# A graph network kernel: the leaky unit of its second edge stage written with tanh, and a group's softmax work spread over two steps

## The reference

```python
def _smooth_leaky(x, alpha=0.2):
    return 0.5 * (1 + alpha) * x + 0.5 * (1 - alpha) * x * (2.0 * jax.nn.sigmoid(x) - 1.0)
ms = src_s[edge_src] + dst_s[edge_dst]          # 64 scalars of an edge
mv = src_v[edge_src] + dst_v[edge_dst]          # 32 vectors of 3
w = h @ rw3 + roff                              # weights of the edge, from an MLP
ds, dv = ...                                    # products of w, ms, mv and the edge's direction Y1
ls, lv = _eq_lin(ds, dv, lin_ws, lin_bs, lin_wv)
alpha = ls[:, :H * A].reshape(e, H, A)          # 8 heads of 8
a = jnp.einsum('ehk,hk->eh', _smooth_leaky(alpha), alpha_dot)
amax = jax.ops.segment_max(a, edge_dst, num_segments=n)
a = jnp.exp(a - amax[edge_dst])
a = a / (jax.ops.segment_sum(a, edge_dst, num_segments=n)[edge_dst] + 1e-12)
ns = jax.ops.segment_sum(vs * a[..., None], edge_dst, num_segments=n)   # and nv likewise
```

## Time and profile before

| | |
|---|---|
| time, median of 3 runs | 10474.15 us (10468.27 to 10480.74) |
| the profiled execution's own time | 10483.94 us |
| its span | 10482.1 us |
| PE busy | 8818.0 us (84%) |
| DVE busy | 7895.4 us (75%) |
| ACT busy | 5096.8 us (49%) |
| POOL busy | 6671.5 us (64%) |
| second edge stage: first and last `e_m` | 5672.5 and 9745.3 us |

### The profile page before, as it was taken

How to read it: one execution, slowest core, us unless ns; L and a number is a source line. 1 busy time by engine, 2 the same in 40 slices (tenths; PEclk the granted TensorE clock), 3 DMA queues, 4 the chain that set the end, 5 groups by cost and what they waited for, 6 DMA issues and landing times. The chain is left out here.

```text
span 10482.1 us, 192677 instructions
## 1 busy us (share of the span) xinstructions
PE 8818.0 (84%) x34728; PEld 5222.1 (50%) x34728; DVE 7895.4 (75%) x15400; ACT 5096.8 (49%) x9268; POOL 6671.5 (64%) x4771
## 2 busy tenths in 40 slices
PE   0888888888888799999996888888888888888588
PEld 0444444444444222322233666676666667676333
DVE  3277777777777588888896888888888888888465
ACT  0176666666666311111112555555555555555355
POOL 4478888888888788888884445444544544444232
PEclk5599999999999899999997999999999999999699
DMA  5588888888888899999993444444444444444222
GB/s 199 180 162 168 167 165 166 166 167 166 168 165 167 171 224 227 230 224 230 225 235 97 124 130 127 124 129 124 126 124 130 126 126 128 125 126 125 67 76 58
DMA packets 1081323, 1616.13 MB, mean 154 GB/s; under 512 B 218498, under 2 KB 831885, under 8 KB 1025357
## 3 DMA queue, kind: packets, MB, share of 16 engines
q1 hardware_dynamic: 755862, 1273.87, 44.1%
q0 software_dynamic: 325056, 338.58, 20.5%
HBM read 1533.80 MB, written 444.07 MB: 189 GB/s over the span
## 5 line engine op out<-in xcount | busy, mean ns | idle before, releaser
L442 POOL DMA_INDIRECT sums<-e_total,e_place x1568 | 2494.2, 1591 | 592.7 <-DMA sums<-e_total,e_place 330.8
L1933 POOL DMA_INDIRECT e_rows<-TS,e_at x1568 | 1540.0, 982 | 2086.2 <-DVE e_m L1961 1334.2
L579 PE MATMUL ps<-e_win,e_pick 128*128 128x448 f32 x3136 | 1335.7, 572 | 168.3 <-DVE e_u L476 127.8
L579 PEld LDWEIGHTS ps<-e_win,e_pick 128*128 128x128 f32 x3136 | 614.1, 201 | 917.3 <-issue 834.0
L2124 PE MATMUL ps<-e_win,e_pick 128*128 128x160 f32 x3136 | 620.7, 324 | 349.3 <-DVE e_pick L1951 281.9
L2261 ACT ACTIVATE e_dT<-ps 128x512 f32<-128x512 f32 x1176 | 660.1, 598 | 372.2 <-PE ps L2135 352.0
L1094 POOL TENSOR_TENSOR n_zv<-n_zv,n_ast 128x1536 f32<-128x1536 f32 x200 | 751.4, 3757 | 134.5 <-DMA n_zv<-in_x_groups 122.7
L2124 PEld LDWEIGHTS ps<-e_win,e_pick 128*128 128x128 f32 x3136 | 487.9, 202 | 564.0 <-issue 403.3
L1299 PE MATMUL ps<-n_z,w_uss 128*64 128x512 f32 x1600 | 746.7, 610 | 22.9 <-DVE n_z L1142 21.9
L2261 ACT ACTIVATE e_oT<-ps 128x512 f32<-128x512 f32 x784 | 468.2, 597 | 603.0 <-PE ps L2163 488.7
L2135 PE MATMUL ps<-ident,e_d 128*128 128x128 f32 x4704 | 648.3, 274 | 125.4 <-ACT e_dT L2261 125.0
(11 more groups left out here) (439 smaller groups left out, 20048.0 us busy)
## 6 DMA issues: line engine op xcount, KB each, us to landing
e_win<-T SPq DMA_DIRECT2D x1568, 168.0 KB
n_z<-in_x_groups SPq DMA_DIRECT2D x400, 512.0 KB
n_zv<-in_x_groups SPq DMA_DIRECT2D x800, 192.0 KB
TOT<-e_tot SPq DMA_DIRECT2D x392, 352.0 KB, 2.6
e_row<-in_src_rows SPq DMA_DIRECT2D x98, 1024.0 KB
e_local<-LR SPq DMA_DIRECT2D x196, 512.0 KB
e_row<-in_dst_rows SPq DMA_DIRECT2D x98, 1024.0 KB
e_win<-TD SPq DMA_DIRECT2D x1568, 60.0 KB
```

Of the source, the lines that this page charges most:

```text
L442: pool.indirect_dma_start(sums[c], bass.IndirectOffsetOnAxis(ap=place[:, r % 4, c:c + 1], axis=0), total[:, r % 4, c, 0:MSG0], None, compu ...
L579: pe.matmul(g[:, c, :], pick[:, p, R * c:R * c + R], win[:, s, c, :], start=True, stop=True).then_inc(spread, 1)
L1933: pool.indirect_dma_start(rows[:, p, 0, c, :], None, TS, bass.IndirectOffsetOnAxis(ap=at[:, gp, col:col + 1], axis=0)).then_inc(rows_here[ ...
```

## The change

Five things change.

1. The silu of `results` becomes a tanh of half the argument; DVE's combination becomes (tanh + 1.5) times alpha instead of 0.25 alpha plus silu, and the constant weight is scaled by 0.4 instead of 0.8. The count and the shapes of the instructions stay.
2. One load of the table set `exp_and_others` stands before the stage's loop on ACT.
3. DVE: `scans` goes from `r % 4 == 0`, behind `weigh`, to `r % 4 == 1`, behind `sums` and ahead of `results`. `shift` goes to behind `weigh` of that same step.
4. PE: `logits_up` stays at the end of `r % 4 == 0`; `tops_down` goes to the next step, behind its last `turn`.
5. ACT: `weigh_up` goes, within `r % 4 == 1`, from ahead of `results` to behind the second `keep_totals`, with only the last `keep` of the step behind it. SP's load of `e_dh`, which waits for the scans, goes from `r % 4 == 1` to `r % 4 == 2`.

```diff
-            step(dve.tensor_scalar(W["ad"][:], W["ad"][:], 0.8, None, ALU.mult))
+            step(dve.tensor_scalar(W["ad"][:], W["ad"][:], 0.4, None, ALU.mult))
...
-                        if r % 4 == 1 and not i.before(4) and not (final and r == 5):
+                        if r % 4 == 2 and not i.before(4) and not (final and r == 6):
                             gate(sp, k)
                             sp.wait_ge(scanned, i.groups(0))
                             load_dh(1 - r // 4, t + r // 4)
...
-                    dve.scalar_tensor_tensor(out=silu[:, p], in0=alpha4, scalar=0.25, in1=silu[:, p], op0=ALU.mult, op1=ALU.add
+                    dve.scalar_tensor_tensor(out=silu[:, p], in0=silu[:, p], scalar=1.5, in1=alpha4, op0=ALU.add, op1=ALU.mult
...
                         if more:
                             sums(after)
+                        if r % 4 == 1 and not i.before(5):
+                            scans(i)
                         if not i.before(1):
                             results(i.plus(-1))
                         if more:
                             weigh(after)
-                        if r % 4 == 0 and not i.before(4):
-                            scans(i)
+                        if r % 4 == 1 and not i.before(5):
                             shift(i)
...
                         turn(i, 2)
+                        if r % 4 == 1 and not i.before(5):
+                            tops_down(i)
                         map_scalars(i)
...
                             logits_up(i)
-                        if r % 4 == 0 and not i.before(4):
-                            tops_down(i)
...
-                    act.activation(silu[:, p], alpha4, ACT.Silu).then_inc(outs, 1)
+                    act.activation(silu[:, p], alpha4, ACT.Tanh, scale=0.5).then_inc(outs, 1)
...
-                        if r % 4 == 1 and not i.before(5):
-                            weigh_up(i)
                         if not i.before(1):
                             results(i.plus(-1))
                         keep(i, 0)
...
                         if not i.before(6):
                             keep_totals(i, 1)
+                        if r % 4 == 1 and not i.before(5):
+                            weigh_up(i)
                         keep(i, 4)
 
+                act.preload_act_table_set("exp_and_others")
```

## The result

The changed kernel takes 10090.11 us (median of 4 runs, 10076.11 to 10095.01), the kernel before, on the same chip, 10471.21 us. The ratio is 0.9626 with a 95% interval of [0.9606, 0.9646]: 381 us less. The forecast was 9961 us with a range of 9930 to 10060, so the direction was right and the time lies 30 us above the range. The profiled execution took 10076.11 us.

A forecast was written before the change was run, and what follows sets the result against it. DVE, with three waits a group, was taken to bound the stage. A group goes from 41.73 to 36.49 us, 5.24 less in each of 98 groups, so 10474 - 513 = 9961 us, range 9930 to 10060.

The forecast's parts named there:

- price of POOL's product: POOL's 1.26 us product waits for the exponential and ends 0.9 us into the next step, before the gathers; cost 0.
- Table loads: ACT in the loop: both loads of each group go, 2.57 us a group, which alone doesn't give the gain.
- Rival C: Scans' waits only moved, so only the table loads' 2.57 us a group came out: 10222 us, chance 0.04.
- ACT's results, scans, maxima: DVE's waits for ACT's copy (310.9 us in all), before the scans (1.22) and before the subtraction (0.56) all go.
- `weigh_up` on ACT: ACT stands 1.8 us for the subtraction; the last `keep` runs 0.6 into the next step, hidden by 0.5 us.
- Rival B: ACT's hold makes the last `keep` late for PE, which would stand 0.8 us a group: 10040 us, chance 0.07.
- the test in the prediction's last part: Step behind scans over 8.64 us refutes the forecast: slow matmuls mean rival A, PE waiting for `e_oT` Rival B.
- Clock: PE idle once a group, 1.5 to 1.7 us behind the long step; no fall 0, one a group 147 us.
- rival A: Clock falls behind PE's new gap: 10108 us if in every group, 10010 if in a third; chance 0.14.
- Rival D: PE loses its clock and doesn't regain it at once; two half-clock steps a group: 10874 us, chance 0.03.
- least group: Scan block on DVE at busy times less overlap, about 1.7 us, gives 25 us more: 9936 us.

The follow-up runs named there:

- subtraction early: Changed kernel with the subtraction of the maxima (`shift`) moved ahead of `weigh`; 10032.09 us, ratio 0.9564; run again 10037.93 us, 0.9557.
- selections first: Kernel with the subtraction early, and `e_pick` also ahead of `e_q` in the scans' step; 10010.93 us, ratio 0.9541; run again 10027.43 us, 0.9545.

## Why the prediction missed

- **What failed is the price of POOL's product.** The prediction wrote that it "is 1.26 us long and ends 0.9 into the next step, ahead of the next gathers", and costed it at 0 because no one waits for it. The place was nearly right (it ends 1.19 into the next step). That it runs beside `e_m` was read off as overlap, and it is none: 1.06 us x 98 = 104 us. In the kernel before, the product met only a part of a short instruction (0.2 us a group, L2027), and I didn't look at which instructions it would meet at its new place. With the product cut to an eighth the group is 36.61 us and the stage 83 us shorter, and the ratio of 0.9552 on 10474.15 us is 10005 us: inside the forecast's range, 44 us above the forecast.
- **Table loads: right that they go, and that they alone don't bring the gain.** Their share is smaller still: 158 us of the stage alone and 7 with the new order, so that the two halves of the change overlap almost wholly, as long as `e_m` is held. Rival C, in which only the loads count, is refuted from both sides.
- **ACT's results, scans, maxima: right.** All three waits of DVE are gone, the step with the scans is 10.57 and 10.44 us in the two groups of a pass against 10.57, and the plain steps have means of 8.60 to 8.65. DVE is above 90% busy.
- **`weigh_up` on ACT: right.** ACT is idle 1.35 and 1.66 us before the exponential in the two groups shown (1.8 forecast), and the copy behind it ends 0.26 into the next step, well before the second half of the window matmuls at 1.52. The list of waits puts PE's gaps down to that `keep` (209.3 us, with a further gap of 0.7 us in the step behind), which the times of `e_pick` contradict. Rival B had the price of what happened and the wrong cause: the test in the prediction's last part, a long step with PE waiting for `e_oT`, would by the list of waits have named B wrongly. Such a test should have been made on the instruction that grew longer.
- **Clock: right for this kernel, but with luck.** PE's gap was forecast at 1.5 to 1.7 us; it is 1.44 in one group and up to 1.81 in the other, with no fall and a clock of 1.00. The forecast took no fall because a gap of 1.5 to 1.7 us is nearer to the 1.12 us of the kernel before behind which the clock stays at 1.00 than to the 3.28 us with a single transpose (7019.38 to 7022.66) behind which it is 0.63. That was weak: the kernel with the subtraction early has falls from 1.84 us on (1 and 12 in 98 groups), which is nearer to 1.12 as well. So rival A holds for the neighbours; the 1.5 us a fall in it are (1 - 0.63) of the 4.00 us of the earlier trace rows. Rival D, the slower one, did not come: in that kernel a fall costs 2.1 us once, and not several steps.
- **Range.** It had room for losses by clock and by ACT, both worked out, and none for two engines that get in each other's way. With the 104 us the same sum gives 10065, 25 below the median measured. (Its least group, with a scan block of 1.7 us instead of 1.93, is worth 23 us and not 25; that changes nothing.)

By stage the account closes: 411.1 us of gain measured, 104 us of held `e_m`, 515 together against a forecast of 513. The median is 14 us above the profiled execution, whose own gain is 10483.94 - 10076.11 = 408; the stages that the change doesn't touch vary by that much, and I can't say why.

## What to carry to other kernels

When an instruction of POOL is moved, look at what DVE does at the new place, not only at who waits for its result: here the product cost nothing beside `e_d`, which reads PSUM (0.55 us as ever), and 1.06 us beside `e_m`, with two tensors in SBUF (1.88 instead of 0.82), and `e_pick` (0.77 instead of 0.48) shows that one tensor in SBUF can be enough. A step forecast from rows of idle time should also list which pairs of instructions become neighbours. And where two edits each remove the same wait (here the loads and the order), test each alone before crediting either; an edit that only shortens a step can lose part of its gain to the clock if the hole in PE's work stays, as the tanh alone did with 86 falls against 42.

## What the runs showed of the hardware

- POOL's product and the DVE instructions with two SBUF inputs that met it excluded each other. `e_m` ends 0.68 to 0.69 us behind the product for products of 0.51, 0.97 and 1.44 us, `e_q` 0.55 us behind it (subtraction early); `e_d`, which reads PSUM and SBUF, keeps its 0.55 us beside it.
- `e_pick`, one bf16 tensor in SBUF and f32 out, is held as well (0.77 us instead of 0.48). Alone, its 512 elements a partition take 0.48 us where those of `e_q` take 0.68; why it is held, no run here shows.
- The wait works both ways: the product takes 1.44 to 1.51 us where it starts during `e_pick` (after), and 1.25 where it starts during `e_d` (subtraction early).
- Tables: exp and silu took a load at every switch, 98 at each of the loop's two lines before, 1283 ns each; exp and tanh take none in the loop, behind one load ahead of it. With the order alone a load of 1.28 us starts at 6540.14 and its silu at 6541.44, 1.30 us later, so the switch shows no price beyond the load.
- The table load did not wait for what its ACTIVATE waits for: with the order alone it starts at 6534.92, and its exponential, held by the subtraction, at 6536.56, 1.64 us later. Two loads a group (2.57 us of ACT) cost 7 us of the stage in all where one fell in idle time and the other ended 0.10 us before its results were needed.
- Two waits of 1.31 and 1.66 us on both sides of one transpose go with a fall of the granted clock to 0.50 in 86 groups with the tanh alone, and the same hole in the kernel before with 42 falls. One wait of 1.84 to 1.91 us goes with one in 1 and 12 groups of 98 (subtraction early), and one of up to 1.81 us (after) or of 1.15 to 1.26 us (selections first) in none.
- The releaser in a bracket is inferred. In after it names ACT's copy at PE's gap, where the times in it and in the kernel with the subtraction early point to DVE's `e_pick`.
